# A hybrid state-space and local-attention kernel on one Trainium2 core: inverse norms by GpSimd's power, two banks for the q/k projections, squares of layer norms on GpSimd, feed-forward steps a turn apart

## The reference

```python
x = x + _L0_attn_a_ref(_layernorm(x), ...)   # state-space mixer A (chunked, 4 heads of 64)
x = x + _L0_ffn_ref(_layernorm(x), ...)      # "layers": 2 layers of local attention + feed-forward
x = x + _L0_attn_b_ref(_layernorm(x), ...)   # state-space mixer B (scan, 16 states)
x = x + _L0_ffn_ref(_layernorm(x), ...)      # the same two layers again
```

```python
h = shift_token(x)                       # half of the features come from the token before
q, k, v = split(h @ wqkv)                # 8 heads of 64
q = q / clip(norm(q), 1e-12) * qs        # l2norm per head; the same for k
k = k / clip(norm(k), 1e-12) * ksc
q, k = rotary_xpos(q, k)                 # q*cos*scale + rotate_half(q)*sin*scale, k with 1/scale
o = local_attention(q, k, v)             # windows of 64 tokens, each looks at itself and the one before
x = x + o @ wo
h = shift_token(x)
h = (h - mean) / sqrt(var + 1e-05) * lg + lb
h = h @ w1 + b1                          # 128 -> 2*341
a, g = split(h); h = a * gelu(g)
x = x + h @ w2 + b2
```

## Time and profile before

| | us |
|---|---|
| median of 3 runs | 2781.34 |
| lowest, highest | 2774.32, 2793.9 |
| the profiled execution | 2801.32 |
| its span (first to last instruction) | 2799.5 |
| mean granted TensorE clock | 0.941 |

### The profile page before, as it was taken

How to read it: one execution, slowest core, us unless ns; L and a number is a source line. 1 busy time by engine, 2 the same in 40 slices (tenths; PEclk the granted TensorE clock), 3 DMA queues, 4 the chain that set the end, 5 groups by cost and what they waited for, 6 DMA issues and landing times. The chain is left out here.

```text
span 2799.5 us, 46444 instructions
## 1 busy us (share of the span) xinstructions
PE 2320.1 (83%) x13516; PEld 1224.0 (44%) x13516; DVE 1919.9 (69%) x5318; ACT 1925.3 (69%) x4833; POOL 1472.8 (53%) x1308
## 2 busy tenths in 40 slices
PE   6999879989999898766776677676799898988987
PEld 3555435545555455412222222222455555555553
DVE  2332357767777676459988998998677676777764
ACT  3444358777777778576877687766687777787774
POOL 1221246555555455247777787676555555555551
PEclk9999979999999999978888888889899999999999
DMA  3000000000000000000000000000000000000000
GB/s 130 1 0 0 0 12 12 13 9 12 13 13 13 9 12 13 5 0 0 1 1 1 0 0 1 0 0 0 12 13 13 9 16 9 13 17 16 20 13 16
DMA packets 12190, 30.46 MB, mean 11 GB/s; under 512 B 2240, under 2 KB 2240, under 8 KB 11456
## 3 DMA queue, kind: packets, MB, share of 16 engines
q1 hardware_dynamic: 11968, 27.99, 3.6%
HBM read 9.11 MB, written 2.10 MB: 4 GB/s over the span
## 5 line engine op out<-in xcount | busy, mean ns | idle before, releaser
L499 POOL TENSOR_TENSOR arena<-arena 128x512 f32<-128x512 f32 x256 | 325.5, 1271 | 691.9 <-DVE arena L1451 689.6
L543 POOL TENSOR_TENSOR arena<-arena 128x512 f32<-128x512 f32 x256 | 328.1, 1298 | 123.9 <-ACT arena L1225 121.3
L1457 DVE TENSOR_REDUCE SM<-arena 128x8 f32<-128x512 f32 x256 | 175.0, 683 | 292.3 <-ACT arena L1093 286.5
L1093 ACT ACTIVATE arena<-psum 128x512 f32<-128x512 f32 x256 | 152.4, 595 | 253.3 <-PE psum L821 249.3
L512 POOL TENSOR_TENSOR P<-P,RS 128x512 f32<-128x512 f32 x256 | 270.2, 1056 | 98.8 <-DVE RS L1383 96.6
L892 PE MATMUL psum<-BS,tabs 96*128 96x512 bf16 x384 | 144.4, 437 | 208.6 <-DVE arena L1534 207.1
L1534 DVE TENSOR_TENSOR_SCAN arena<-arena,psum 128x512 f32<-128x512 f32 x256 | 310.9, 1215 | 3.2
L961 PE MATMUL psum<-arena,first 128*128 128x512 f32 x512 | 290.4, 656 | 11.2 <-POOL arena L534 10.9
L821 PE MATMUL psum<-rest,HA 128*128 128x512 f32 x512 | 273.5, 616 | 11.7 <-DVE arena L1451 10.6
L505 POOL TENSOR_TENSOR arena<-arena,SR 128x512 f32<-128x512 f32 x256 | 275.2, 1075 | 7.4 <-ACT SR L1103 6.5
L774 PE MATMUL psum<-HN,rest 128*128 128x512 f32 (+1 forms) x384 | 195.0, 620 | 94.6 <-DVE arena L1418 45.6
(11 more groups left out here) (222 smaller groups left out, 5816.5 us busy)
## 6 DMA issues: line engine op xcount, KB each, us to landing
arena<-arena SPq DMA_DIRECT2D x128, 128.0 KB, 2.3
rest<-in_rest SPq DMA_DIRECT2D x1, 4183.0 KB, 22.6
X<-in_x SPq DMA_DIRECT2D x1, 2048.0 KB, 10.6
out<-X SPq DMA_DIRECT2D x8, 256.0 KB, 2.2
first<-in_first SPq DMA_DIRECT2D x1, 1445.5 KB, 6.2
tabs<-in_tabs SPq DMA_DIRECT2D x1, 1216.0 KB, 13.1
```

What stands on the lines that cost most here:

```text
L499: nc.gpsimd.tensor_tensor(CQ[:, n % 2, :], CQ[:, n % 2, :], SQN[:, n % 2, :], ALU.add).then_inc(f_rope, 1)
L543: nc.gpsimd.tensor_tensor(WU[:, k % DEEP, :], RG[:, k % DEEP, :], U[t.j % 2][:, k % 2, :], ALU.mult).then_inc(m_wu, 1)
```

## The change

Inverse norms: ACT's `norms` (Ln, Exp) is gone; in POOL's `scaled` one tensor_tensor with the power operation raises the 128x8 sums to -0.5 and then the multiplication follows. Squares of the inner and outer norms in the layers stages go from ACT to POOL (end of g = 2 and g = 0). Projections of q go to bank 4, those of k to bank 5; O_BANK, the output of `weigh`, moves to the upper half of bank 0, whose lower half `scores` uses, and `weigh` gets a wait on `maxima`. Gelus move behind `squares`, and PE's steps of the feed-forward part move. The copies XC are gone: PE and DVE read x itself, and PE gets waits at the beginnings of stages in their place.

```diff
-        S_BANK, P_BANK, O_BANK = (bank[0], bank[1]), bank[2], bank[4]
-        QK_BANK, T_BANK, V_BANK = bank[5], bank[6], bank[3]
+        S_BANK, P_BANK, O_BANK = (bank[0], bank[1]), bank[2], bank[0][:, 256:512]
+        QK_BANK, T_BANK, V_BANK = (bank[4], bank[5]), bank[6], bank[3]
...
             def scaled(k, m, n):
+                k.wait_ge(f_ss, 8, n + 1, slot=m)
+                nc.gpsimd.tensor_tensor(SR[:, n % 2, :], SS[:, n % 2, :], power_col[:, :].to_broadcast([128, HEADS]),
+                                        ALU.pow).then_inc(f_sr, 1)
                 k.wait_ge(f_rope, 8, n + 1, slot=m)
                 k.wait_ge(f_sr, 8, n + 1, slot=m)
...
+            def square_centred(wait, norm, centred, square):
+                wait(norm.cen)
+                nc.gpsimd.tensor_tensor(square, centred, centred, ALU.mult).then_inc(norm.sq, 1)
...
+                    if k.outer and g == 0:
+                        square_centred(outer_at, outer, CEN2[:, :], LSQ2[:, :])
+                    if k.post and g == 2:
+                        square_centred(inner_at, inner, CEN[:, :], LSQ[:, :])
...
                 if h == 1:
-                    t.wait_ge(ln_in, 1, 1, pair=1)
                     t.wait_ge(a_xt, 4, 4)
-                    mm(X_BANK[1], F("mean128"), XC[:, :], start=True, stop=True).then_inc(ln_mean, 1)
+                    mm(X_BANK[1], F("mean128"), X[:, t.tokens(1)], start=True, stop=True).then_inc(ln_mean, 1)
...
-                k.wait_ge(f_prod, 8, n, slot=m)
-                mm(QK_BANK, HA[k.side(m)][:, 128 * tt:128 * tt + 128],
+                k.wait_ge(f_prod, 8, n - 1, slot=m)
+                mm(QK_BANK[n % 2], HA[k.side(m)][:, 128 * tt:128 * tt + 128],
...
-                    elif h == 13:
+                    elif h == 14:
                         inner_var(k)
                     elif h == 17:
                         gate_half(k, 0)
                         gate_half(k, 1)
-                    elif h == 18:
+                    elif h == 21:
                         gate_half(k, 2)
-                    elif h == 21:
                         other_half(k, 0)
-                    elif h == 22:
+                    elif h == 25:
                         other_half(k, 1)
                         other_half(k, 2)
-                    elif h in (25, 26, 27):
-                        down_projection(k, h - 25)
+                    elif h == 29:
+                        for m in range(3):
+                            down_projection(k, m)
...
                     if k.heads(g - 1):
+                        if k.heads(g + 1):
+                            k.wait_ge(f_nb, 16, 2 * k.heads(g + 1)[1] + 1, slot=k.heads(g + 1)[0])
                         weigh(k, *k.heads(g - 1))
...
-            def norms(k, m, n):
-                k.wait_ge(f_ss, 8, n + 1, slot=m)
-                A(SL[:, n % 2, :], SS[:, n % 2, :], ACT.Ln, scale=SS_SCALE).then_inc(f_sl, 1)
-                k.wait_ge(f_sl, 8, n + 1, slot=m)
-                A(SR[:, n % 2, :], SL[:, n % 2, :], ACT.Exp, bias=unscale_col[:, :], scale=-0.5).then_inc(f_sr, 1)
...
-                if k.post and h == 12:
-                    square_centred(inner, inner_at, CEN[:, :], LSQ[:, :])
...
-                if k.post and h == 18:
-                    gelus(k)
                 if item(k, h, 1):
                     squares(k, *item(k, h, 1))
+                if k.post and h == 19:
+                    gelus(k)
...
-                if k.ahead and h == 10:
+                if k.ahead and h == 11:
                     shift_ahead(k)
-                if k.outer and h == 0:
-                    if k.j > -2:
-                        k.wait_pair(outer.cen, 1)
-                    TS(XC[:, :], X[:, k.tokens(2)], 1.0, None, ALU.mult).then_inc(outer.ready, 1)
...
-                    elif h == 11:
+                    elif h == 10:
                         centre(inner, inner_at, HF[:, :], STAT, CEN[:, :])
...
-                    elif h == 23:
+                    elif h == 26:
                         gated(k, 1)
                         gated(k, 2)
-                    elif h == 29:
+                    elif h == 31:
                         after_feed_forward(k)
```

More of the change, by code:

```diff
@@ L513, in proportions, with inner_at, outer_at @@
                                         ALU.mult).then_inc(f_rp, 1)
+            def square_centred(wait, norm, centred, square):
+                wait(norm.cen)
+                nc.gpsimd.tensor_tensor(square, centred, centred, ALU.mult).then_inc(norm.sq, 1)
             def pool_slot(k):
+                def inner_at(semaphore):
+                    k.wait_ge(semaphore, 1, 1, slot=-1)
+                def outer_at(semaphore):
+                    k.wait_pair(semaphore, 2)
                 for g in range(8):
@@ L805, in outer_mean @@
             def outer_mean(k):
-                k.wait_pair(outer.ready, 2)
                 if k.j > -2:
@@ L809, in outer_mean @@
                 k.wait_ge(f_r2, 1, 1, slot=-2)
-                mm(STAT, F("mean128"), XC[:, :], start=True, stop=True).then_inc(outer.mean, 1)
+                mm(STAT, F("mean128"), X[:, k.tokens(2)], start=True, stop=True).then_inc(outer.mean, 1)
             def outer_var(k):
@@ L988, in _ @@
             pairs(pe, pe_turn)
+            pe.wait_ge(m_x, PAIRS)
             layers_pe(1)
@@ L1071, in flipped @@
                 A(PT[:, g % 2, :], P_BANK, ACT.Copy).then_inc(f_pta, 1)
-            def square_centred(norm, wait, centred, square):
-                wait(norm.cen)
-                A(square, centred, ACT.Square).then_inc(norm.sq, 1)
             def inverse_root(norm, wait, variance, root):
@@ L1092, in squares @@
                 k.wait_ge(f_rope, 8, n - 1, slot=m)
-                A(SQN[:, n % 2, :], QK_BANK, ACT.Square).then_inc(f_sq, 1)
+                A(SQN[:, n % 2, :], QK_BANK[n % 2], ACT.Square).then_inc(f_sq, 1)
             def values(k, tt):
@@ L1455, in sums @@
                 k.wait_ge(f_sq, 8, n + 1, slot=m)
-                k.wait_ge(f_sl, 8, n - 1, slot=m)
                 v.reduce_sum(SM[:, n % 2, :], SQN[:, n % 2, :].rearrange("p (h d) -> p h d", d=DH), AX.X).then_inc(f_sm, 1)
@@ L1468, in outer_at @@
                     k.wait_pair(semaphore, 2)
-                if k.ahead and h == 10:
+                if k.ahead and h == 11:
                     shift_ahead(k)
-                if k.outer and h == 0:
-                    if k.j > -2:
-                        k.wait_pair(outer.cen, 1)
-                    TS(XC[:, :], X[:, k.tokens(2)], 1.0, None, ALU.mult).then_inc(outer.ready, 1)
                 if k.outer and h == 2:
-                    k.wait_pair(outer.ready, 2)
-                    centre(outer, outer_at, XC[:, :], STAT, CEN2[:, :])
+                    centre(outer, outer_at, X[:, k.tokens(2)], STAT, CEN2[:, :])
                 if k.outer and h == 7:
```

40 lines of the change are left out of this document (11 added, 29 removed).

## The result

The change makes the kernel slower: 2991.12 us (median of 4 runs, 2987.83 to 2994.48) against 2784.88 (4 runs, 2774.32 to 2793.9), a ratio of 1.0731, with a 95% interval of [1.0703, 1.076]. The forecast was 2737, its range ended at 2860. Ratios are of fast runs alone, which matters for the copies-alone kernel: one of its six runs was a slow one of 7389.8 us, and its ratio leaves that run out.

The account below looks back on a forecast made before the run. PE was taken as the bound in mixer A and the layers, DVE in mixer B. Layers 22 us and copies 22 us off 2801.3 gave 2757, or 2737 us on the median; range 2660 to 2860.

Parts of the forecast that it names:

- c: Cost of one power operation in POOL's list, taken as 0.4 us, the nearest row (a 128x128 tile).
- group 1: Its transposes in a layers slot, whose item crosses the light group: forecast 0.04 us + c late.
- group 5: Its transposes in a layers slot, behind the later variance and `flip` behind `proportions`: forecast 0.6 us + c.
- group 6: Its transposes in a layers slot, after exponentials made late by the gelus: forecast c - 0.1 us.
- the fourth place: A fourth wait in each layers slot, growing beyond c = 0.56 us, by c - 0.56.
- formula: Gain of a layers slot: 1.95 - 3c us, less a further c - 0.56 beyond c = 0.56.
- the power is dear: Rival: power in POOL's list between `proportions` and `scaled` makes it slower, 2840 us at c = 1.3; chance 0.27.
- gain of 1.95 us a slot: Layers slot of 48.4 us becomes 46.45 + 3c, so 1.95 us is gained before the power's cost.
- The gelu stall: At the head of group 6, a new 2.4 us wait at `weigh` replaces two of 1.67 and 1.73.
- at nothing: Items priced at zero: `weigh`'s new wait, two banks, ACT's shorter list, waits at the stage beginnings.
- The copies: Removing copies of x gains 13 us in mixer A, 7 in mixer B, 2 at starts of layers stages.
- third rival: All stalls in the layers go, PE runs without waits: 169 us gained, 2612 us; chance 0.1.

Follow-up runs that it names:

- copies-alone kernel: The kernel before with only the copies of x taken away: 2776.13 us, 0.9921.
- third-bank kernel: The changed kernel with norms on ACT, feed-forward steps and gelus at old places, one q/k bank, the freed bank for third hidden tiles: 2676.96 us, 0.9595.
- the power alone: The kernel before with only the inverse norms moved to POOL's power: 2961.86 us, 1.0584.
- the power off: The changed kernel with the inverse norms back on ACT (Ln, Exp), all else as changed: 2780.79 us, 0.9954.
- the stall alone: The third-bank kernel with only the feed-forward steps and gelus at the places of the change: 2793.42 us, 1.0002.
- the power earlier: The changed kernel with the clip ahead of all products on DVE and the power ahead of `rotated` on POOL: 2818.83 us, 1.01.
- third-bank kernel with the power: The third-bank kernel with the inverse norms by POOL's power again, nothing else changed: 2906.18 us, 1.0402.
- the steps back: The changed kernel, power still in, with feed-forward steps, gelus and gated steps at their old places: 2935.11 us, 1.0501.

## Why the prediction was wrong

**The price of the power, the first step that failed.** The prediction bounded c "by the nearest rows", 0.14 to 1.27, and took 0.4 from a multiply of 128 columns. It measured 1.67. The lower rows could not say it, since they were of an operation 96 times cheaper a column, and the upper one, "as if each of the 8 elements cost 64 plain ones", was no bound either: eight columns at 0.16 us come to 1.27 by themselves, and the 0.4 us of fixed cost stands on top. The prediction itself says "The trace has no power operation", and then let two bounds from plain operations close the range at 2860, at a power of 1.4 us. The range had to stay open upwards.

**The path held, the places of the waits in part.** The prediction put c on the item's path behind `proportions`, uncovered in three places of a slot and in a fourth beyond 0.56. At c = 1.67 its terms are 1.71 us before the transposes of group 1, 2.27 in group 5, 1.57 in group 6 and 1.11 in the fourth place. The slot shown has 1.65 in group 1, 0.71 in group 5 and 0.25 in group 6, and 1.42 and 0.72 in groups 3 and 4. Group 1 came out, and the fourth place can be group 3 or 4; groups 5 and 6 are far smaller than forecast, and 4.75 us in all are less than the formula's 6.66. I read this as waits that cover one another, since a PE that has waited once comes later to the next transposes; no run separates it. POOL's occupation hardly mattered: with as many powers on it, only in another order, the kernel wins back 172 of the power's 210 us. The rival "the power is dear" was the right one. Its formula at 1.67 is 1.95 - 5.01 - 1.11 = -4.2 us a slot, 125 us in all, and 2781 + 125 - 22 = 2884. The measured time lies 107 above that.

**The clock, the second step, not in the sum at all.** The prediction read a clock of 1.00 in the layers and kept it for the slot to come, although it foresaw a PE stall of 2.4 us where none had been above 1.6. That stall came at 2.59, and PE's busy time of the slot rose by 2.96 us for the same 344 matmuls. Over the two stages it rose by 92 us (45.0 and 47.1), and the idle time by another 92, where the formula has 125 of waits. So slower matmuls put 92 on and smaller waits took 33 off. The third-bank kernel with only the stall added shows that the stall brings the slow clock: 45 us more of PE's busy time over both stages. It is not the only source: the power alone, whose waits before the transposes are of 0.3 to 2.2 us, raised the busy time by 63.

**The change without the power.** Its gain of 1.95 us a slot was to be 58 us in all, but the two stages with the power off took 6.8 us longer and 0.7 shorter than before, so that 64 us are missing, 2.1 a slot. PE's busy time rose by 29 us there, 1.0 a slot. Its idle time fell by 23 us, 0.8 a slot, instead of 58. Part of these missing 35 can be named: the stall at `weigh` was taken at 2.4 and costs 2.7 a slot, the maxima cost 5.4 us before `weigh`, where the forecast had nothing, and the hidden tiles still wait 5.1. The rest I have not followed.

**The number of slots.** The sum counted 15 slots a stage, those between two inner means. The powers stand in all slots that make q/k items. Beside the 90.7 and 93.8 us of the two stages, the stretch between them shows 1.7 us more than before, where the copies alone took 18 off it, and the first inner mean comes 6.1 us later, where the copies alone brought it 8.3 forward. That is some 34 us beyond the counted slots. The stretch between the stages varies, though: 850.1 to 867.4 us in the profiled executions of five kernels with neither power nor copies, 876.1 to 879.8 in three with the power at its place in the change and no copies. So 92 - 33 + 34 is 93 of the 107. The rest is for the most part the base: the forecast took 20 us off its profiled execution to come to the median, and the changed kernel's profiled execution lies only 3 above its median.

**The outer square.** The prediction had POOL's square of the outer norm make its variance later "by about what that gives back" and counted nothing for it. With a power ahead of it, the outer variance waits 23.6 us in the whole kernel, where it waited 3.0; single waits reach 2.48 us. With the power off it is 5.7.

**What was right.** The gelu stall: 2.4 forecast, 2.59 measured, at the head of group 6, released by ACT's copy. No wait before the inner variance, gate tile 2 or other tile 2 in the slot shown; in the last two slots of a stage the inner variance still waits, 4.5 us in all. Of the waits taken "at nothing", the new one of `weigh` on the maxima shows 5.1 us in six places, where `scores` showed 2.4 before. The copies: 22 us forecast, 22 measured, but that the total came out is luck: in mixer A 13 was too much, since ACT's step (L661) waited next, and in mixer B 7 too little, since there DVE is the bound and 10.4 us of its work went. The inner squares on POOL: 0 forecast, and within the interval 0 in the third-bank kernel.

**What the stalls were worth.** The third rival's "all stalls go", given 0.1, priced 4.9 us a slot and 2612 us. With a bank of its own for the third hidden tile and the steps at their old places a slot is 45.1 us and the kernel 2676.96; most of the stalls could be had, but not by moving the steps.

## What to carry to other kernels

An operation that no row of the trace shows has no upper bound from rows of other operations: keep the range open above it, or ask first whether the path it stands on can take several times its guessed price. Place it by the item's path and not by the engine's load: the same 256 powers cost 210 us behind the products and 38 ahead of them. The same engine's list can hold up a second consumer, as the outer variance here. And sum PE's stalls by their length as well as by their total, since one long stall in a dense stream can cost half as much again in slow matmuls behind it.

## What the runs showed of the hardware

- GpSimd's power costs 0.16 us a column of 128 partitions and 0.4 fixed: 1.65 us for 8 columns, 20.7 for 128. The Trainium skill ("GPSIMD Engine Reference", "Engine selection") wants elementwise work kept off this engine. The rows agree for the power, which cost 229 us in the third-bank kernel; for the squares of the layer norms they do not, since 0.9595 and 0.9592 are the same. Both comparisons are with ScalarE; none here is with VectorE.
- A PE stall of 2.59 us makes a spell at the lower clock likely and not certain. In the layers stages such a stall had a spell with it (begun between 0.7 us ahead of the stall's end and 2.2 behind it) 26 times of 27 in the changed kernel, 24 of 28 with the stall alone, 21 of 28 with the power off and 17 of 28 with the power earlier. Stalls of 1.9 to 2.5 us had one 29 times of 37 in the power-alone kernel, 25 of 28 in the third-bank kernel with the power and 11 of 28 with the steps back. Stalls of 1.4 to 1.9 us had one 39 times of 330 in all eleven kernels, those of 0.6 to 1.4 us once in 446. The spells lasted some 3 to 10 us. What decides between stalls of one length stays open.
